# A gated cross-attention layer on one core: low parts of queries read from PSUM, low parts of keys made by GpSimd, other split buffers, another order on SyncE

## What is computed

```python
x = x + tanh(g_xattn) * attention(layernorm(x), ctx)     # 16 heads of 32, biases, softmax over 120 keys
h = layernorm(x)
x_scale = max(abs(h), per token) / 127                   # at least 1e-6 / 127
x_q = clip(round(h / x_scale), -128, 127)                # int8
x = x + tanh(g_ffn) * ((x_q @ weight_q.T) * x_scale * weight_scale + bias)
```

## Time and profile before

| | us |
|---|---|
| median of 3 runs | 806.0 |
| lowest, highest | 805.67, 806.8 |
| the profiled execution | 809.15 |
| its span, first to last instruction | 807.0 |
| TensorE busy in it | 769.5 |
| ScalarE, VectorE, POOL busy | 610.1, 584.6, 533.8 |

### The profile page before, as it was taken

How to read it: one execution, slowest core, us unless ns; L and a number is a source line. 1 busy time by engine, 2 the same in 40 slices (tenths; PEclk the granted TensorE clock), 3 DMA queues, 4 the chain that set the end, 5 groups by cost and what they waited for, 6 DMA issues and landing times.

```text
span 807.0 us, 16228 instructions
## 1 busy us (share of the span) xinstructions
PE 769.5 (95%) x5835; PEld 531.2 (66%) x5890; DVE 584.6 (72%) x879; ACT 610.1 (76%) x844; POOL 533.8 (66%) x524
## 2 busy tenths in 40 slices
PE   9896999999999999999999999999999989999996
PEld 6664467667666766766676676667667657666563
DVE  5864778677776857777686777768578796756568
ACT  5774668778687877868788786878778677787785
POOL 4836348485775948577595857759485765855588
PEclk9998999999999999999999999999999999999998
DMA  8899897879888887878878798788879757746722
GB/s 284 298 311 247 212 272 212 248 212 261 239 225 246 222 265 211 258 227 236 251 225 235 216 258 250 219 248 228 251 218 264 213 161 242 208 151 185 202 67 104
DMA packets 119519, 183.21 MB, mean 227 GB/s; under 512 B 37648, under 2 KB 47248, under 8 KB 117392
## 3 DMA queue, kind: packets, MB, share of 16 engines
q1 hardware_dynamic: 92368, 133.33, 54.2%
q10 hardware_dynamic: 27072, 48.84, 23.6%
HBM read 123.91 MB, written 58.22 MB: 226 GB/s over the span
## 4 chain that ended last, share of the span: by engine, by line
PE 75%; DVE 7%; DMA 6%; issue 5%; POOL 3%; ACT 3%; SPq 1%; ACTq 1%; DVEq 0%; POOLq 0%
PE bank_b L437 25%; PE bank_a L437 15%; PE scores L492 7%; PE scores L511 6%; PE sum_ps L519 6%; PE pv_ps L523 6%; PE bank_a L567 4%; DMA q_rows<-q_parts 2%; DVE row_max L1228 2%; PE scores L437 1%; PE bank_a L542 1%; PE bank_b L567 1%; DMA q_stack<-q_rows 1%; DMA x_in<-in_x 1%; SPq L232 1%
## 5 line engine op out<-in xcount | busy, mean ns | idle before, releaser
L1584 POOL TENSOR_TENSOR o_lo<-on,o_hi 128x512 fp32r<-128x512 f32 x48 | 64.6, 1346 | 135.9 <-ACT o_hi L907 135.9
L1228 DVE TENSOR_REDUCE row_max<-scores 128x16 f32<-128x1920 f32 x64 | 137.7, 2151 | 10.3 <-PE scores L492 10.3
L1239 DVE TENSOR_TENSOR q_parts<-q_sb,q_parts 128x512 fp32r<-128x512 f32 x60 | 64.3, 1072 | 111.4 <-ACT q_parts L851 111.4
L889 ACT ACTIVATE probs<-scores 120x2048 f32<-120x2048 f32 x64 | 120.0, 1876 | 18.8 <-PE scores L511 18.6
L1540 POOL TENSOR_TENSOR xt<-xt,rstd_b 128x512 f32<-128x512 f32 x60 | 97.8, 1665 | 6.8 <-DMA xt<-in_x_t 5.8
L492 PEld LDWEIGHTS scores<-k_sb,q_sb 32*128 32x128 f32 x1984 | 61.0, 186 | 51.9 <-issue 44.4
L1580 POOL TENSOR_TENSOR x<-x,gbo_r 128x512 f32<-128x512 f32 x64 | 93.6, 1474 | 0.6 <-DMA x<-in_x 0.5
L1592 POOL TENSOR_TENSOR x<-x,gbias_r 128x512 f32<-128x512 f32 x64 | 83.2, 1302 | 15.7 <-ACT cen L913 14.7
L511 PE MATMUL scores<-q_stack,k_stack 128*120 128x512 f32 x256 | 73.0, 406 | 12.5 <-DVE row_max L1228 8.7
L1597 POOL TENSOR_TENSOR x<-x,u_sb 128x512 f32<-128x512 f32 x56 | 74.2, 1324 | 7.1 <-DVE u_sb L1320 7.0
L437 PE MATMUL bank_b<-xt_hi,wq_hi 128*128 128x512 f32 x188 | 77.0, 409 | 1.2 <-DVE xt_lo L1218 1.2
(11 more groups left out here) (235 smaller groups left out, 1927.5 us busy)
## 6 DMA issues: line engine op xcount, KB each, us to landing
q_stack<-q_rows ACTq DMA_DIRECT2D x183, 256.0 KB, 4.3
q_rows<-q_parts SPq DMA_DIRECT2D x61, 512.0 KB, 4.5
xt<-in_x_t SPq DMA_DIRECT2D x16, 1024.0 KB, 8.7
x<-in_x SPq DMA_DIRECT2D x64, 256.0 KB, 4.2
out_x<-x SPq DMA_DIRECT2D x61, 256.0 KB, 2.3
x_in<-in_x SPq DMA_DIRECT2D x60, 256.0 KB, 5.1
k_stack<-k_rows SPq DMA_DIRECT2D x96, 120.0 KB, 4.4
k_rows<-k_parts SPq DMA_DIRECT2D x28, 240.0 KB, 2.2
```

The costliest lines, as they stand in the source:

```text
L889: act.activation(probs[0:KEYS], scores[0:KEYS], ACT.Exp, scale=SCALE).then_inc(p_ready, 1)
L1228: dve.tensor_reduce(row_max[:].rearrange("p (t r) j -> p r t j", r=ROWG)[:, :, :, j], scores[:, :, 0:QT * KEYS].rearrange("p r (t k) -> p ...
L1584: pool.tensor_tensor(o_lo[i % 2][j], on[:], o_hi[i % 2][j].bitcast(F32), ALU.subtract).then_inc(o_split, 1)
```

## The change

- **Buffers.** One `q_sb` in place of two, two `q_parts` in place of one; `q_parts` alternates with j%2, for batch 0 the blocks 2 and 3 borrow other tiles. `split_high` waits for the landing of the store of block j-2 (of the batch before for j < 2). `bias_q` waits for no low part any more, but for the first block.
- **Low parts of queries** (`split_low`): VectorE reads the projection out of its bank, adds the bias and subtracts the high part in one instruction. So the bank is in use until then, and TensorE gets four waits on `q_split` per step ahead of instructions that write the bank again.
- **Low parts of keys**: POOL makes all of them (`low_k`), two per step, one after `add_out(e, 2)`, one after `low_o(i, 2)`; VectorE none.
- **SyncE**: another order ahead of the loop; `load_rstd(2)` and `load_xt(2)` go from the end of it into step 0, behind `store_q(1, 1)`.
- **ScalarE**: in step 0 the high part of query block 1 goes ahead of the rounding of the output weights; `high_o(0, j)` waits for low parts of batch 0, whose queries lie in the same tiles.
- **POOL ahead of the loop**: low parts in another order, and it waits for the split of x of batch 1 before the low parts of query blocks 2 and 3.
- **Maxima**: `max_sp` is compact, its windows for the four turns overlap. In step 14 VectorE makes their low parts ahead of `dequantise`, and TensorE turns them before the last part of `project_o(m, 3)`. In step 0 the low part of x, `low_x(2, 0)`, goes ahead of `fold_rows`.

```diff
-        q_sb = [sb(f"q_sb{i}", [P, S]) for i in range(2)]
-        q_parts, k_parts = sb("q_parts", [P, 2, S], F32R), sb("k_parts", [P, 2, KEYS2], F32R)
+        q_sb = sb("q_sb", [P, S])
+        q_parts = [sb(f"q_parts{i}", [P, 2, S], F32R) for i in range(2)]
+        k_parts = sb("k_parts", [P, 2, KEYS2], F32R)
...
         def q_parts_of(n, j):
-            if n == 0 and j == DT - 1:
-                return o_hi1[:, 2], o_lo1[:, 2]
-            tile = q_parts if n > 0 or j == 0 else (o_hi1, o_lo1)[j - 1]
-            return tile[:, 0], tile[:, 1]
+            return [o_lo1, o_hi1][j - 2][:, 0:2] if n == 0 and j >= 2 else q_parts[j % 2][:]
...
             load_xt(1)
             load_ctx(1)
+            store_k(0, 0)
+            store_q(0, 0)
             load_x(2, 0)
-            store_k(0, 0)
             store_k(0, 1)
-            store_q(0, 0)
+            stack_q(0, 0)
             load_x(2, 1)
             stack_k(0, 0)
-            stack_q(0, 0)
             store_q(0, 1)
+            load(rest_landed, u_sb[:].bitcast(I32), rows(wq8))
+            stack_q(0, 1)
+            load_x(2, 2)
+            store_q(0, 2)
+            load_x(2, 3)
             store_k(0, 2)
             store_k(0, 3)
-            load(rest_landed, u_sb[:].bitcast(I32), rows(wq8))
-            stack_q(0, 1)
-            stack_k(0, 1)
-            store_q(0, 2)
             store_q(0, 3)
-            load_x(2, 2)
-            load_x(2, 3)
             load(rest_landed, gbo_r[:], bo.partition_broadcast(P))
             stack_q(0, 2)
             store_q(1, 0)
+            stack_k(0, 1)
...
             store_rstd(2)
-            load_rstd(2)
-            load_xt(2)
 
             def step(i):
...
                 if is_batch(b):
                     store_q(b, 1)
                 if i == 0:
+                    load_rstd(2)
+                    load_xt(2)
                     load_x(f, 2)
...
                 if i > 0 and b % 2 == 1:
                     pe.wait_ge(v_ready, nth(b, 1))
+                if keys_next or values_next and i > 1 or not is_batch(n):
+                    pe.wait_ge(q_split, nth(b - 1, DT, 0))
                 if is_batch(e):
                     quantised_layer(e, 1, bank_a if is_batch(n) else bank_b)
...
+                pe.wait_ge(q_split, nth(b - 1, DT, 0))
                 project_q(b, 1, bank_b)
...
                 if is_batch(m):
+                    pe.wait_ge(q_split, nth(b - 1, DT, 1))
                     project_o(m, 1, bank_b)
...
+                pe.wait_ge(q_split, nth(b - 1, DT, 2))
                 if i == 0:
                     project_k(pair, 2, bank_a)
                     project_k(pair, 3, bank_a)
...
+                pe.wait_ge(q_split, nth(b - 1, DT, 3))
+                if is_batch(m) and i < LAST - 1:
                     project_o(m, 3, bank_b)
+                if i == LAST - 1:
+                    for c in range(DT - 1):
+                        add_heads(m, 3, c, bank_b)
...
                 turn_max(b, sum_ps)
+                if i == LAST - 1:
+                    add_heads(m, 3, DT - 1, bank_b).then_inc(proj_done, 1)
...
             def bias_q(n, j, bank):
-                act.wait_ge(*split_of(n - (j < 2), (j + 2) % DT))
+                if n == 1 and j == 0:
+                    act.wait_ge(q0_split, 1)
...
-                if n == 1 and j == 0:
-                    act.wait_ge(q_stored[0], stores_of(0, 0))
-                elif n > 0:
-                    act.wait_ge(q_stored[(j - 1) % DT], stores_of(n - (j == 0), (j - 1) % DT))
-                act.activation(q_parts_of(n, j)[0], q_of(n, j), ACT.Copy).then_inc(q_hi_done, 1)
+                if n > 0 and j >= 2:
+                    act.wait_ge(q_stored[j - 2], stores_of(n))
+                if n == 1 and j < 2:
+                    act.wait_ge(q_stored[j], stores_of(0))
+                if n > 1 and j < 2:
+                    act.wait_ge(q_stored[j + 2], stores_of(n - 1))
+                act.activation(q_parts_of(n, j)[:, 0], q_of(n, j), ACT.Copy).then_inc(q_hi_done, 1)
...
+                if i == 0 and j < DT - 1:
+                    act.wait_ge(q0_split, j + 2)
                 act.activation(o_hi[i % 2][j], on[:], ACT.Copy).then_inc(o_hi_done, 1)
...
-            def split_low(n, j):
+            def split_low(n, j, bank):
                 dve.wait_ge(q_hi_done, nth(n, DT, j))
-                dve.tensor_tensor(q_parts[:, 1], q_of(n, j), q_parts[:, 0].bitcast(F32), ALU.subtract).then_inc(q_split, 1)
-
-            def split_low_k(pair, j):
-                dve.wait_ge(k_hi_done, nth(pair, DT, j))
-                parts = k_parts_of(pair, j)
-                dve.tensor_tensor(parts[:, 1], k_sb[pair % 2][:, j], parts[:, 0].bitcast(F32),
-                                  ALU.subtract).then_inc(k_split, 1)
+                parts = q_parts_of(n, j)
+                dve.scalar_tensor_tensor(out=parts[:, 1], in0=bank[:], scalar=bq_c[:, j:j + 1], in1=parts[:, 0].bitcast(F32),
+                                         op0=ALU.add, op1=ALU.subtract).then_inc(q_split, 1)
...
+            def low_k(pair, j):
+                pool.wait_ge(k_hi_done, nth(pair, DT, j))
+                parts = k_parts_of(pair, j)
+                pool.tensor_tensor(parts[:, 1], k_sb[pair % 2][:, j], parts[:, 0].bitcast(F32),
+                                   ALU.subtract).then_inc(k_split, 1)
...
                 if is_batch(e):
                     add_out(e, 2)
+                if is_batch(k_of(i)):
+                    low_k(k_of(i) // 2, 2 * (i % 2))
...
                 low_o(i, 2)
+                if is_batch(k_of(i)):
+                    low_k(k_of(i) // 2, 2 * (i % 2) + 1)
...
+            low_k(0, 0)
             for c in range(CT):
                 pool.wait_ge(wv_hi_done, c + 1)
                 pool.tensor_tensor(wv_lo[:, c], wv_stage[:, c], wv_hi[:, c].bitcast(F32), ALU.subtract).then_inc(wv_lo_done, 1)
-            low_k0(0)
-            low_k0(1)
-            low_q0(0)
+                if c == 0:
+                    low_q0(0)
+            low_k(0, 1)
             x_rstds(1)
             low_q0(1)
             for c in range(DT):
                 scale_x(1, c)
+            pool.wait_ge(x_split, nth(1, DT, 3))
             low_q0(2)
+            low_k(0, 2)
+            low_k(0, 3)
             low_q0(3)
```

More of the change, by code:

```diff
@@ L193, in q_of, with stores_of @@
         def q_of(n, j):
-            return u_tail[:, j - 1] if n == 0 and j >= 2 else q_sb[j % 2][:]
-        def stores_of(n, j):
-            return 16 * (n + 1 + (j == DT - 1))
+            return u_tail[:, j - 1] if n == 0 and j > 0 else q_sb[:]
+        def stores_of(n):
+            return 16 * (n + 1)
         def split_of(n, j):
@@ L278, in store_q @@
                     sp.wait_ge(q_stacked[j % 2], 48 * nth(n - 1, 2, j // 2))
-                if n == 0 and j == DT - 1:
-                    for part, tile in enumerate(q_parts_of(n, j)):
-                        sp.dma_start(q_rows[j, part], tile.bitcast(F32)).then_inc(q_stored[j], 16)
-                else:
-                    both = q_parts if n > 0 or j == 0 else (o_hi1, o_lo1)[j - 1]
-                    sp.dma_start(q_rows[j].rearrange("h p s -> p h s"), both[:, 0:2].bitcast(F32)).then_inc(q_stored[j], 16)
+                sp.dma_start(q_rows[j].rearrange("h p s -> p h s"), q_parts_of(n, j).bitcast(F32)).then_inc(q_stored[j], 16)
             def stack_q(n, j):
-                sp.wait_ge(q_stored[j], stores_of(n, j))
+                sp.wait_ge(q_stored[j], stores_of(n))
                 if n > 0 or j >= 2:
@@ L294, in store_k @@
             def store_k(pair, j):
-                if pair == 0 and j < 2:
-                    sp.wait_ge(k0_split, j + 1)
-                else:
-                    sp.wait_ge(k_split, nth(pair, DT, j) - 2)
+                sp.wait_ge(k_split, nth(pair, DT, j))
                 if pair > 1:
@@ L499, in turn_max @@
                 for t in range(QT):
-                    ins = pe.matmul(bank[:, t * P:(t + 1) * P], max_sp[:, t], ident_r[:], start=True, stop=True)
+                    ins = pe.matmul(bank[:, t * P:(t + 1) * P], max_sp[:, t * DH:t * DH + P], ident_r[:], start=True, stop=True)
                 ins.then_inc(max_turned, 1)
@@ L1544, in low_q0 @@
                 pool.wait_ge(q_hi_done, nth(0, DT, j))
-                high, low = q_parts_of(0, j)
-                pool.tensor_tensor(low, q_of(0, j), high.bitcast(F32), ALU.subtract).then_inc(q0_split, 1)
-            def low_k0(j):
-                pool.wait_ge(k_hi_done, nth(0, DT, j))
-                parts = k_parts_of(0, j)
-                pool.tensor_tensor(parts[:, 1], k_sb[0][:, j], parts[:, 0].bitcast(F32), ALU.subtract).then_inc(k0_split, 1)
+                parts = q_parts_of(0, j)
+                pool.tensor_tensor(parts[:, 1], q_of(0, j), parts[:, 0].bitcast(F32), ALU.subtract).then_inc(q0_split, 1)
+            def low_k(pair, j):
[3 more added lines that the diff above has]
```

(1 more changed line is left out.)

47 lines of the change are left out of this document (22 added, 25 removed).

## The result

The changed kernel takes 812.7 us (median of 4, 812.14 to 812.89), the kernel before beside it 806.4: a ratio of 1.0077, 95% interval 1.006 to 1.0095. It is slower by 6.3 us, where 803.6 was forecast, and outside the range. When it was run again (first experiment) the ratio was 1.0042 (1.0022 to 1.0062).

The account below looks back on a forecast made before the run. TensorE was taken as the bound, busy 527.68 of 535 us from 105 to 640 us. Median 806.0 - 3.6 (step 0) - 1.1 (stall) - 0.7 (step 14) + 3.0 (new waits) = 803.6 us; range 797.0 to 811.5.

Parts of the forecast that it names:

- the gain of step 0: First pass of the main loop (batch 0): ScalarE's 7.14 us wait goes, 3.6 us gained, bounds 0.5 and 9.5.
- the landing of the deviations: Batch 0's pass: the stored deviations still land at 65.1 us, since the queue carries the same bytes before them.
- the delay of the key store by ScalarE's loads: Batch 0's pass: three ScalarE loads come earlier and may delay the store by 0 to 3.1 us; taken as 0.
- The steady loss: Later passes: TensorE's new waits for low parts of queries lose 3.0 us, bounds 0 and 6.7.
- some 4: Batch 0's pass, ScalarE's key split: a new idle stretch of some 4 us, ended by the store of split keys.
- Lands at 77.7: Batch 0's pass: the key store lands at 77.7 us instead of 79.7, one query store (2.0 us) being gone.
- nothing is left: Rival, chance 0.17: ScalarE's loads precede the key store, it lands at 80.8, batch 0's pass gains 0.5: 806.7 us.
- The waits of TensorE: Block 0, before the quantised layer: five odd batches at 0.40, 2.0 us; batch 3 0.7; block 2 0.3.
- hidden in both forms: Steady passes: VectorE's time for low parts, old or new form, lies hidden under TensorE.
- The stall of step 12: Batch 12's pass: TensorE's 2.23 us wait behind a 6.61 us key part goes; half counted, 1.1 us gained (0 to 2.2).
- Step 14: End of batch 14's pass: reordered low maxima come earlier and shorten TensorE's 1.36 us wait, 0.7 us gained (0 to 1.4).
- The port: Rival, chance 0.19: POOL takes the shared port before VectorE's last low parts of x, priced at 8: 811.6 us.

Follow-up runs that it names:

- first experiment: The changed kernel, unaltered, timed again on another chip beside the kernel before: 810.7 us against 807.6, ratio 1.0042.
- second profile: Profile of the changed kernel, unaltered, from its repeat on another chip: 810.7 us, ratio 1.0042 to the kernel before.
- the run with both moves: Changed kernel with key blocks 2 and 3 of the first pair early and pair 1's first key store ahead of the deviations' load: 805.1 us, 0.9988.
- three single edits of the changed kernel: Changed kernel with one edit each: early keys 2 and 3 (1.0021), key store ahead of the deviations (1.0001), block 0's wait behind the quantised layer (1.0026).
- four edits together: Changed kernel with early keys, key store first, block 0's wait behind the quantised layer, and VectorE's x statistics later: 797.0 us, 0.987; again 798.0, 0.9895.

## Why the prediction was wrong, point by point

**The step that failed** is the gain of step 0: 3.6 us were forecast, with bounds of 0.5 and 9.5 that leave no room for a loss, and the step got 3.8 us longer (4.8 in the second profile). Three of its terms were wrong: the moved loads of keys, put at nothing; the landing of the deviations, kept at 65.1; and the delay of the key store by ScalarE's loads, taken as 0. The steady loss was mis-sized besides.

**The diagnosis held.** The 7.14 us on ScalarE went, and the key split became the wait that takes its place, as written: 5.44 us instead of "some 4", before the attention of block 3.

**The moved load that wasn't walked.** Ahead of the loop, the loads of keys for blocks 2 and 3 went behind nine other entries of SyncE's queue, from 43.95 in the kernel before to 52.47 us, the last landing at 66.0:

```profile
43.95 1.29 SPq L232 DMA_DIRECT2D k_stack<-k_rows  x3
```

The prediction costed the front's new order at nothing and followed only the deviations through it. The 6.06 us wait and its slow clock have no term and no rival there. With these keys early the wait is gone, and with GpSimd's part of that alone it stays at 5.89: SyncE's place has to change for it to go.

**"Before the deviations the queue carries the same bytes in another order, so I keep 65.1."** They landed at 68.8: SyncE reached their store 1.46 us later, and it took 11.0 instead of 8.8 us. Two groups of loads had moved ahead of it: the keys of the last paragraph, and three loads of stacked queries (0.79 MB) that ScalarE issues behind block 1, whose high part now comes earlier. These went out at 55.71 us, before at 59.23, behind the store at 56.29:

```profile
59.23 1.30 ACTq L808 DMA_DIRECT2D q_stack<-q_rows  x3
```

Which group makes how much is not separated. With the keys early again, two of ScalarE's loads ahead of the store (55.15) and the third right behind it, the store took 7.8 us, so those loads alone don't explain it; with SyncE's old order and ScalarE's loads at 54.86 it took 10.8, so the moved keys alone don't either.

**The key store.** "Lands at 77.7" was 84.0: 3.7 us by the deviations, 0.4 up to the issue, and 2.3 because it took 11.4 us from issue to landing and not 9.1. The 2.0 us for the query store that is no longer in between did come, nearly: the issue follows the deviations by 3.9 us instead of 5.5. What did not hold is "I take 0" for the three loads that ScalarE issues after the split of block 2: they went out at 72.94, beside the key store. Of the nine profiles in which the key store stands behind the loads of x, the seven with ScalarE's loads within 5 us of it have 9.1 to 11.4 us, and the two with them over 7 us earlier 7.0 and 7.3; no run moved these loads alone.

With SyncE's old order the key store landed at 79.6, and the stretch lost 0.2 us, near the rival "nothing is left" with its gain of 0.5. So without the new order the rest of the change brings nothing in step 0, where the prediction put 3.6. With it, the first attention of step 1 starts 2.4 us later than before, although the 1.2 us of waits for low parts of x, which lie ahead of it, are gone as forecast. A gain of 1.4 us in the rest of step 1, where three waits of the kernel before for maxima and for a copy on ScalarE went (0.9 us), was not forecast.

**The waits of TensorE.** The place and the batches were right, odd ones from 5 on and none in even ones; the size was not: 0.70 instead of 0.40. Left out was the time from the end of the low part to the start of the released weight load, 0.22 us; most of the rest is the 0.05 that stays when the wait is moved. Five times 0.7 is 3.5 instead of 2.0. Batch 3, priced at 0.7, lost 0.26 at this wait, and 1.05 just ahead of it, where the turned maxima came late (0.89 us, in this execution; in the second profile 0.75 in all). The whole term: 3.0 forecast, 5.7 measured from step 1's last block to step 12's (4.8 in the second profile).

**VectorE's time "is hidden in both forms"** holds for key parts of their usual length, and not where something ahead of a low part is held up. TensorE now waits for low parts, so what stands ahead of them on VectorE can count: in step 0 a wait for x and the gating of two rows cost 4.33 us (the run with both moves), and with the key parts back on VectorE the two long ones cost most of 4.5 us. The Trainium skill (GPSIMD Engine Reference, section 4.1) gives elementwise work on a tile to VectorE; here the kernel with these parts on VectorE was the slower one, in its trace by the two long parts. The low part itself took 0.717 to 0.752 us in all 60, as forecast.

**The stall of step 12.** Half of it was taken off the median. Of four profiles with the loop's key parts on VectorE one shows it in step 12, one in step 2, two not at all, and the profile with it in step 12 lies 2.75 us above its kernel's median. That would fit timed runs that mostly lack it, and then the 1.1 us were too much. But of the two profiles without it one (`load_rstd(2)` and `load_xt(2)` moved) lies 3.8 us below its kernel's median, so how often the timed runs have it stays open. The Trainium skill (SBUF — State Buffer, "Who interferes with whom") has the loser of the shared port wait for the whole instruction of the other engine; the second case, 6.62 us beside five operations, again differs.

**Step 14**: 0.7 forecast, 0.52 measured. **The port**: its price, 811.6, lay near the result, but not its mechanism; the three low parts of x took 2.54 to 2.60 instead of 2.39 us in the steady steps, and even batches lost nothing. That the price came near was luck.

The sum again with the measured terms: against the median, and with the stall of step 12 counted as nothing, +2.4 to step 1's first attention, -1.4 in step 1, +5.7 to step 12, -0.5 in step 14 make 6.2, and 6.3 was measured. The fit is closer than it can be relied on: the +2.4 holds a start of step 0 that came 1.4 us earlier, and the same sum from the second profile makes 4.9, where 3.1 was measured. Had step 0 gained its 3.6 us and the rest come as measured, it would have been 806.4 - 3.6 + 5.7 - 0.5 = 808.0, or 806.6 with the 1.4 us of step 1. With the steady loss of 3.0 as forecast and the rest as measured it would have been 806.4 + 2.4 - 1.4 + 3.0 - 0.5 = 809.9. Either miss alone would have lost the forecast gain.

## What to carry to other kernels

A queue written out by hand has to be walked entry by entry: for each transfer that is moved, find who waits for its landing, not only the one transfer that the change is about. In a stretch where the DMA queue is full, waits stand in a chain, and taking one away pays only when the next two are seen and moved with it: the new buffers with SyncE's old order, the changes of order on the old buffers, and three single edits of the changed kernel each ended within 0.3% of the kernel before (two more, of GpSimd's part alone and of the key parts on VectorE, at 0.7 and 1.0% above it), and four edits together 1.0 to 1.3% below it. When a wait on another engine is added, add the release time to its lateness, and ask of everything ahead of the awaited instruction what happens when it is late or held up.

## What the runs showed of the hardware

In the changed kernel a key store of 240 KB took 11.4 us from issue to landing behind some 2 MB of loads issued in the 4 us before it (72.67), and 2.1 us for the next block, when nearly nothing else moved (85.31). A VectorE subtraction with two operands in SBUF, 0.375 us at best, took 6.6 us twice and 5.7 us once while GpSimd ran operations on end, at three places in two of four profiles and never over 1.2 us in the other two; that GpSimd is what holds it up is read from this overlap and was not tried. From the end of VectorE's low part to the start of the weight load that waits for it some 0.22 us pass, in each of the five steps. And the first attention of step 0 started anywhere from 44.2 to 48.1 us in the fourteen profiles, 3 us apart for kernels with the same order there; what sets this was not found. These 3.9 us stand beside a spread of 6.9 us of single executions in one set of the kernel before (802.4 to 809.3).
